# Cross-attention with layer norm: scores from high and low query parts, masks converted once and spread through DRAM

## The reference

```python
Q, K, V = heads(x @ wq.T + bq), heads(ctx @ wk.T + bk), heads(ctx @ wv.T + bv)
scores = where(mask == 0, -1e9, Q @ K.T / 4)
out = (softmax(scores) @ V).merged() @ wo.T + bo + x
out = (out - mean) * rsqrt(var + 1e-5) * gamma + beta
```

## Time and profile before

| what | value |
|---|---|
| median of three runs | 165.19 us (164.49, 165.19, 167.47) |
| the profiled execution's own time | 164.33 us |
| its span | 162.5 us |
| busy in the span: PE / DVE / ACT / POOL | 137.3 / 124.9 / 94.7 / 115.5 us |
| mean granted TensorE clock | 0.964 of full |

### The profile page before, as it was taken

The page is one execution under the profiler, slowest core; times in us unless marked ns, Lnnn a source line. Parts: engine busy times, 40 slices in busy tenths (PEclk is TensorE's granted clock), DMA queues, the critical chain, the costliest instruction groups (busy, mean ns, idle before and its releaser), DMA issues.

```text
span 162.5 us, 2904 instructions
## 1 busy us (share of the span) xinstructions
PE 137.3 (84%) x992; PEld 87.0 (54%) x992; DVE 124.9 (77%) x231; ACT 94.7 (58%) x166; POOL 115.5 (71%) x111
## 2 busy tenths in 40 slices
PE   0798975989899998999899989998999579999400
PEld 0676853746556655565556565655665335468300
DVE  0263899348788897989798979898989797999951
ACT  3349687593963666766676675846763815640220
POOL 5003741029999539999999999999981899667783
PEclk9999999699999999999999999999999999999955
DMA  4988983999927886006730940048003503003024
GB/s 119 342 234 198 283 197 85 317 244 269 287 71 187 314 217 252 0 0 196 180 148 0 224 167 0 2 105 274 12 2 76 187 0 129 0 4 122 7 94 166
DMA packets 10175, 23.21 MB, mean 143 GB/s; under 512 B 1584, under 2 KB 1840, under 8 KB 10160
## 3 DMA queue, kind: packets, MB, share of 16 engines
q1 hardware_dynamic: 9584, 22.03, 46.7%
q10 hardware_dynamic: 576, 0.99, 1.9%
HBM read 14.62 MB, written 4.19 MB: 116 GB/s over the span
## 4 chain that ended last, share of the span: by engine, by line
PE 45%; DVE 15%; POOL 14%; issue 7%; DMA 7%; SPq 6%; ACT 3%; POOLq 1%; DVEq 0%
PE ps_w L436 11%; PE ps_w L357 9%; PE ps_w L331 8%; DMA m_sb<-maskT 7%; PE ps_s L385 6%; PE ps_s L412 5%; POOL y L873 5%; DVE nmax L667 4%; POOL y L876 4%; DVE turned L688 3%; SPq L215 3%; PE ps_s L391 3%; ACT y L585 2%; DVE cn L701 2%; POOL rstd L857 2%
## 5 line engine op out<-in xcount | busy, mean ns | idle before, releaser
L667 DVE TENSOR_REDUCE nmax<-ps_w 128x8 f32<-128x512 f32 x56 | 37.7, 678 | 15.2 <-PE ps_w L357 14.8
L572 ACT ACTIVATE probs<-ps_s 128x512 f32<-128x512 f32 x64 | 33.1, 602 | 18.3 <-PE ps_s L396 18.3
L810 POOL TENSOR_TENSOR xt_l<-xt_sb,xt_h 128x1024 fp32r<-128x1024 f32 x7 | 16.6, 2374 | 30.6 <-ACT xt_h L533 19.8
L436 PE MATMUL ps_w<-wo_sb,cn 128*128 128x256 f32 x112 | 29.3, 387 | 3.9 <-DVE cn L701 3.6
L357 PEld LDWEIGHTS ps_w<-k_half,q_mask 128*128 128x128 f32 x112 | 17.3, 190 | 25.5 <-DVE nmax L667 19.7
L357 PE MATMUL ps_w<-k_half,q_mask 128*128 128x256 f32 x112 | 27.9, 335 | 3.2 <-DVE nmax L667 2.9
L436 PEld LDWEIGHTS ps_w<-wo_sb,cn 128*128 128x128 f32 x112 | 19.3, 189 | 9.2 <-DVE cn L701 5.5
L585 ACT ACTIVATE y<-res,shift,rstd 128x256 f32<-128x256 f32 x28 | 14.8, 590 | 12.6 <-POOL shift L859 12.5
L873 POOL TENSOR_TENSOR y<-y,brow 128x512 f32<-128x512 f32 x14 | 17.9, 1279 | 4.5 <-ACT y L585 4.1
L688 DVE STREAM_TRANSPOSE turned<-ps_s 128x1024 f32<-128x1024 f32 x16 | 19.8, 1240 | 0.8 <-PE ps_s L412 0.8
L844 POOL TENSOR_TENSOR x_sb<-x_sb,brow 128x1024 f32<-128x1024 f32 x8 | 19.1, 2382 | 0.1
(11 more groups left out here) (75 smaller groups left out, 203.3 us busy)
## 6 DMA issues: line engine op xcount, KB each, us to landing
m_sb<-maskT SPq DMA_DIRECT2D x32, 128.0 KB, 3.5
q_mask<-mask SPq DMA_DIRECT2D x32, 128.0 KB, 2.6
x_sb<-x SPq DMA_DIRECT2D x8, 512.0 KB, 4.3
xt_sb<-xT SPq DMA_DIRECT2D x7, 512.0 KB, 4.4
out<-y SPq DMA_DIRECT2D x6, 512.0 KB, 3.4
xt_sb<-xT SPq DMA_DIRECT2D x2, 256.0 KB, 5.7
out<-xt_sb SPq DMA_DIRECT2D x2, 256.0 KB, 2.0
brow<-bias_rows SPq DMA_DIRECT2D x1, 384.0 KB, 6.4
```

The lines of the kernel that those rows point to most:

```text
L436: return pe.matmul(tile_outputs(c, i)[:, t], cn[:, c % 2, j, (2 * i + t) * P:(2 * i + t + 1) * P], wo_sb[:, j], start=j == 0 and c < LAST, ...
L572: act.activation(probs[:, g % 2, quad], ps_s[:, quad], ACT.Exp).then_inc(e_done, 1)
L667: dve.tensor_reduce(nmax[:, c % 2, t].rearrange("p (q r) -> p q r", r=32)[:, :, 2 * j:2 * j + 2], max_bank(c, i).rearrange("p (q h k) -> p ...
```

## The change

- **Masks of chunks 3 to 7.** They are loaded once (64 keys, as two halves of the queries on 128 partitions by 256 columns), converted by one VectorE instruction in step s for chunk s + 3, behind divide(s - 1, 1) and ahead of maxima 4; written to a tensor `masks` in DRAM, and read back from there to `mask` (four transfers) and to `q_mask` (two). GpSimd's `mask_values` is gone, and so are `load_mask` and `copy_mask` for these chunks.
- **Mask of chunk 0** comes in a second copy (`m_first`) that VectorE writes straight into `q_mask`, by two instructions; `copy_mask(0)` is gone. Mask 2 and the value blocks move on VectorE behind maxima(1, 2) of step 0.
- **Scores from chunk 2** use high and low parts of queries and keys, as float32r: three products of four quads each in place of the float32 product. The high parts are ACT copies (`queries_high` twice a chunk, `keys_high` once), the low parts GpSimd differences (`queries_low`, `keys_low`).
- **Values** are projected per batch and per head parity, 16 float32 products of 64 x 128 in place of 8 of 128 x 256, all ahead of max_scores(0, 0); the bias is added by two instructions in place of five.
- **ACT** makes the high part of chunk 1 ahead of the first queries. **SP** loads xT(1) and wv ahead of mask 0.
- **Ends:** in TensorE's step 7 output(5, 1) stands ahead of values(6, 1); on VectorE moments(5, 0) come behind maxima(7, 7), and residual and moments (5, 1) ahead of divide(6, 1); on GpSimd the last chunk's first deviations come ahead of deviations(6, 2:4).

```diff
@@ -214,6 +238,31 @@
                     sp.dma_start(m_sb[quad_rows(quad), c % 2], maskT[c].rearrange("(a k) n -> k a n", a=2)
                                  ).then_inc(in_mask[c % 2], 16)
+
+            def load_once(c):
+                if c >= SPREAD_FROM + 2:
+                    sp.wait_ge(once_done, c - 1 - SPREAD_FROM)
+                for u in range(2):
+                    sp.dma_start(m_once[rows(u), c % 2], maskT[c, :, u * COLS:(u + 1) * COLS]).then_inc(in_once[c % 2], 16)
+
+            def mask_away(c):
+                sp.wait_ge(once_done, c + 1 - SPREAD_FROM)
+                for u in range(2):
+                    sp.dma_start(masks[c, :, u * COLS:(u + 1) * COLS], mask_once[rows(u), c % 2].bitcast(F32)
+                                 ).then_inc(mask_out[c % 2], 16)
+
+            def spread_mask(c):
+                n = (c - SPREAD_FROM) // 2 + 1
+                sp.wait_ge(mask_out[c % 2], 32 * n)
+                sp.wait_ge(max_done, HALVES * (c - 1))
+                for half in range(2):
+                    sp.dma_start(q_mask[rows(1 - half), c % 2, half].bitcast(F32),
+                                 masks[c].unsqueeze(1).to_broadcast([64, 2, CHUNK])).then_inc(beside_in[c % 2], 16)
+                if c >= NM:
+                    sp.wait_ge(s_done, PAIRS * (c - NM + 1))
+                for quad in range(QUADS):
+                    sp.dma_start(mask[quad_rows(quad), c % NM].bitcast(F32),
+                                 masks[c].rearrange("(a k) n -> k a n", a=2)).then_inc(mask_in[c % 2], 16)
...
@@ -245,10 +294,11 @@
             load_first_xt(0)
             load_first_xt(1)
+            for half in range(2):
+                sp.dma_start(m_first[rows(half)], maskT[0]).then_inc(in_mfirst, 16)
+            load_xt(1)
+            sp.dma_start(wv_sb[:], wv).then_inc(in_wv, 16)
             load_mask(0)
-            sp.dma_start(wv_sb[:], wv).then_inc(in_wv, 16)
-            load_xt(1)
-            copy_mask(0)
             load_mask(1)
...
@@ -259,16 +309,19 @@
             sp.dma_start(brow[:, 1:4], bias_rows[:, 1:4].to_broadcast([P, 3, D])).then_inc(in_rows, 16)
             sp.dma_start(wo_sb[:], wo).then_inc(in_wo, 16)
-            load_mask(3)
+            load_once(3)
             load_xt(4)
-            load_mask(4)
+            load_once(4)
             load_x(1)
+            mask_away(3)
             for s in range(1, CHUNKS):
                 if s + 4 < CHUNKS:
                     load_xt(s + 4)
-                    load_mask(s + 4)
+                    load_once(s + 4)
                 if s + 2 < CHUNKS:
-                    copy_mask(s + 2)
+                    spread_mask(s + 2)
+                if s + 3 < CHUNKS:
+                    mask_away(s + 3)
                 if s + 1 < CHUNKS:
...
@@ -287,18 +340,20 @@
                     for d in range(PC):
                         mm = pe.matmul(ps_w[:, 1, j * 256:j * 256 + 256], wk_sb[:, d, j * P:(j + 1) * P],
-                                       ctx_t[:, d, 0:BATCHES], start=d == 0, stop=d == PC - 1)
+                                       ctx_t[:, d], start=d == 0, stop=d == PC - 1)
                 mm.then_inc(k_done, 1)
-            def project_values(b):
-
-                if b == 0:
-                    pe.wait_ge(in_wv, 16)
-                for d in range(PC):
-                    mm = pe.matmul(value_bank(b)[:, 0, (b % 2) * 256:(b % 2) * 256 + 256],
-                                   ctx_t[:, d, b:b + 2].rearrange("p b k -> p (b k)"), wv_sb[:, d],
-                                   start=d == 0, stop=d == PC - 1)
-                mm.then_inc(v_done, 1)
+            def project_values():
+
+                pe.wait_ge(in_wv, 16)
+                for b in range(BATCHES):
+                    for d in range(PC):
+                        for h in range(2):
+                            mm = pe.matmul(projected_values(h)[:, b], ctx_t[:, d, b],
+                                           wv_sb[:, d].rearrange("p (q e) -> p q e", e=32)[:, :, 16 * h:16 * h + 16],
+                                           start=d == 0, stop=d == PC - 1)
+                            if d == PC - 1:
+                                mm.then_inc(v_done, 1)
...
@@ -380,11 +440,26 @@
                     pe.wait_ge(qe_done, g + 1)
                     pe.wait_ge(e_done, QUADS * g)
-                for quad in range(QUADS):
-                    r = quad_rows(quad)
-                    pe.matmul(ps_s[:, quad], k_pair[r, b, j].rearrange("p h k -> p (h k)"), q_sb[r, c % NQ, j],
-                              start=True, stop=False)
-                pe.wait_ge(mask_done, c + 1)
+                if c < PARTS_FROM:
+                    for quad in range(QUADS):
+                        r = quad_rows(quad)
+                        pe.matmul(ps_s[:, quad], k_pair[r, b, j].rearrange("p h k -> p (h k)"), q_sb[r, c % NQ, j],
+                                  start=True, stop=False)
+                else:
+                    pe.wait_ge(kh_done, 1)
+                    pe.wait_ge(kl_done, 1)
+                    pe.wait_ge(qh_done, g + 1 - 2 * PARTS_FROM)
+                    for n, (k, q) in enumerate(((k_high, q_high), (k_low, q_high), (k_high, q_low))):
+                        if q is q_low:
+                            pe.wait_ge(ql_done, g + 1 - 2 * PARTS_FROM)
+                        for quad in range(QUADS):
+                            r = quad_rows(quad)
+                            pe.matmul(ps_s[:, quad], k[r, b, j].rearrange("p h k -> p (h k)"), q[r, c % 2, j],
+                                      start=n == 0, stop=False)
+                if c < SPREAD_FROM:
+                    pe.wait_ge(mask_done, c + 1)
+                else:
+                    pe.wait_ge(mask_in[c % 2], 16 * QUADS * ((c - SPREAD_FROM) // 2 + 1))
                 for a in range(2):
...
@@ -460,11 +535,8 @@
             project_keys()
             project_first_queries()
-            project_values(0)
-            project_values(1)
-            project_values(2)
+            project_values()
             max_scores(0, 0)
-            project_values(3)
             max_scores(0, 1)
...
@@ -477,9 +549,9 @@
                 scores(s, 0)
                 if s == LAST:
-                    values(LAST - 1, 1)
                     output(LAST - 2, 1, 0)
                     output(LAST - 2, 1, 1)
+                    values(LAST - 1, 1)
                     scores(LAST, 1)
...
@@ -612,6 +693,8 @@
                 if s < LAST:
                     queries_beside(s + 1, 1)
+                if PARTS_FROM <= s + 1 < CHUNKS:
+                    queries_high(s + 1, 1)
                 if s == 0:
...
@@ -624,6 +707,9 @@
                 if s + 2 < CHUNKS:
                     queries_beside(s + 2, 0)
+                    if s == 0:
+                        keys_high()
+                    queries_high(s + 2, 0)
                 if s == LAST:
...
@@ -669,16 +755,15 @@
             def value_blocks():
-                dve.wait_ge(v_done, BATCHES)
+                dve.wait_ge(v_done, 2 * BATCHES)
                 dve.wait_ge(fill_done, 5)
                 dve.wait_ge(in_bv, 16)
-                for h, b, n, first in ((0, 0, 2, 0), (0, 2, 2, 2), (1, 0, 2, 1), (1, 2, 1, 3), (1, 3, 1, 0)):
+                for h in range(2):
                     r, e = rows(h), slice(16 * h, 16 * h + 16)
                     dve.tensor_tensor(
-                        v_bd[r, first:first + n, :, e],
-                        value_bank(b)[r, 0].rearrange("k (b p e) -> k b p e", b=2, e=32)[:, b % 2:b % 2 + n, :, e],
+                        v_bd[r, :, :, e], projected_values(h),
                         brow[r, 0].rearrange("k (p e) -> k p e", e=32)[:, :, e].unsqueeze(1)
-                        .to_broadcast([64, n, PAIRS, 16]), ALU.add).then_inc(vbd_done, 1)
+                        .to_broadcast([64, BATCHES, PAIRS, 16]), ALU.add).then_inc(vbd_done, 1)
...
@@ -734,13 +819,28 @@
             def scaled(i):
                 c = LAST
-                dve.wait_ge(ln_done, deviations_done(LAST - 1, True) + 2 * (i + 1))
+                dve.wait_ge(ln_done, deviations_done(c, i == 1))
                 dve.wait_ge(beta_done, 1)
                 dve.wait_ge(last_gam_done, 2 * (i + 1))
                 for t in (2 * i, 2 * i + 1):
                     dve.scalar_tensor_tensor(y_of(c)[:, t], y_of(c)[:, t], rstd[:, c % 2, t:t + 1], beta(),
                                              ALU.mult, ALU.add).then_inc(last_bet_done, 1)
+            def first_mask_values():
+                dve.wait_ge(in_mfirst, 32)
+                for half in range(2):
+                    r = rows(1 - half)
+                    dve.tensor_scalar(q_mask[r, 0, half], m_first[r].unsqueeze(1).to_broadcast([64, 2, CHUNK]), 0.0, -BIG,
+                                      ALU.is_equal, ALU.mult).then_inc(mfirst_done, 1)
+
+            def mask_values_once(c):
+                n = (c - SPREAD_FROM) // 2
```

(55 more changed lines are left out.)

53 lines of the change are left out of this document (42 added, 11 removed).

## The result

The changed kernel takes 181.33 us (median of four, 180.78 to 182.49) against 165.34 for the kernel before on the same chip: a ratio of 1.0995, 95% interval 1.0915 to 1.1075. The prediction was 179.0 us, with slower at 0.93. The profiled execution took 181.49 us, its span is 179.7, so 17.2 us have come on top of the 164.33 of the one before.

A forecast was written before the change was run, and what follows sets the result against it. It took a loop through VectorE and TensorE, 16.21 us a step, as the bound. From 164.33, -0.95 + 8.2 + 4.8 + 0.5 + 2.2 gave 179.1, say 179.0 us; range 171 to 185.

The forecast's parts named there:

- Mask 3 in step 0: VectorE's first `mask_values_once` waits for mask 3, issued late on SP's queue: loss 6.5 us, +8.2 with clock and front.
- quick landing: Rival: mask 3, 128 KB in place of 512, lands quickly; +8.2 falls to +2.8, total 173.7 us; chance 0.12.
- The front: Up to the first scores: no `copy_mask(0)` wait and values in column pairs give -0.7 us (bounds -1.5, +0.5).
- Half clock: After step 0's stall, TensorE works another 3.41 us stretch at a granted clock of 0.50: +1.7 us.
- Conversions beside GpSimd: Steps 1 to 4: VectorE's mask conversion waits for GpSimd's instruction to end, +4.8 us (bounds 0.4 and 10).
- The rival that nobody holds them: GpSimd does not hold the conversions; steps cost 0.4 us, step 0 is 0.7 shorter, total 174.0; chance 0.13.
- The masks' way through DRAM: DRAM round trip of masks 4 to 7 has most of a step before it is read: 0 us.
- Scores in parts: Float32r rounds save TensorE 0.38 us a group, 4.6 over twelve; -0.95 us reaches the end (bounds 0, -4.6).
- TensorE is not the bound: Denies the rival that TensorE is the bound and all 4.6 us reach the end, 175.4; chance 0.11 with tail.
- `neg` late by 0.5: Half_keys in step 4 make deviations(2) late, and ACT's normalising then holds `neg` up: +0.5 us (bounds 0, 2).
- GpSimd's tail and the ends: GpSimd's list from step 6 ends later, +2.2 us (bounds 0, +3); the other ends count 0 (-1, +1).
- Other side: Rival: mask 3 is there near 29.6, step 0 has no stall, -4.0 for +8.2, total 166.9 us; chance 0.04.

## Why the prediction was right

**Mask 3 in step 0: right, and undersized.** Predicted for start and step 0 together +8.2, measured 11.0. The way was as written: mask 2 later, SP's copies later, mask 3 issued at 35.03 (predicted 32.3), landed at 42.16 (39.4), conversion held by low_x(3) for about a microsecond (1.03; predicted 1.1), first scores of step 1 at 49.48 (46.7). Of the 2.8 us between the two, 1.7 were there when mask 2 was done (29.43 against 27.7), and the rest is the queue, where mask 3 follows mask 2 by 5.6 in place of 4.65. Moving it ahead of the copies, moving mask 2's copies behind it, and doing mask 2 earlier each took its share of step 0 away (9.9, of which 5.2 came back in step 1, 8.6 and 3.7 us of the 24.94). The bound of +2.8 for a quick landing leaves out the conversion itself, 0.35; nothing hung on it.

**The front: the step that failed.** I took -0.7 for everything up to the first scores; it was +1.1. Mask 0 stands on VectorE where GpSimd has just started low_x(1): 2.71 us in place of 0.69. I had read just that from mask 2, used it for steps 1 to 4 and not here, where a `low_x` was in GpSimd's list as well. A half-clock stretch at 17.4 came on top. The runs part the two: with neither the start is 21.9 to 22.1 (mask 0 moved, or begun ahead of low_x), with mask 0 held and no stretch 22.8 to 23.5, with both 24.4 to 25.0. So the rest of the front gave 1.4, twice what I took, the held conversion cost some 0.9 and the stretch, which no run explains, 1.6.

**Half clock: +1.7 predicted, about 2.2 measured.** The stretch lasted 13.65 us, but TensorE was busy for only 4.31 us of them (the last of the stretches above), so half of that, 2.2, was lost. The cost was nearly right, the picture of one more 3.41 us stretch was not, and in part it was luck: the old stretch at 28.03, which I had left standing, was gone (1.6 us of loss less), and the one at 17.4, which I had not in the sum, cost 1.7.

**Conversions beside GpSimd: right.** The predicted extra in steps 1 to 4 was 0.59, 0.59, 1.79, 1.79, less 0.19 each for scores: 0.4, 0.4, 1.6, 1.6 against +0.3, +0.1, +1.5, +1.5. Steps 3 and 4 are named by TensorE's wait for VectorE (1.41 us at 93.74) and by the 2.02 and 2.04 us. The rival that nobody holds them is out: the durations of one instruction follow those on GpSimd, a swap on GpSimd alone took both steps back to 16.0 and 16.3, and where VectorE began first it was GpSimd's instruction that became longer. The masks' way through DRAM, taken as 0, was 0: no wait in the changed kernel is put down to a landing from `masks`.

**Scores in parts: -0.95 predicted, about -0.4 measured.** The chain shows what TensorE spends on a group, three rounds and the mask's:

```profile
133.25 0.91 PE ps_s L457 x8
134.16 0.46 PE ps_s L466 x6
```

The three rounds take 0.91 in place of 1.07: 0.16 saved a group, not 0.38, about 2 us over twelve groups and not 4.6. I had priced a round at 0.23 from the mask's. Of it 0 to 0.2 us a step reach the end, 0.4 over steps 2 to 5. TensorE is not the bound: a step with 0.35 us less of its work was at most 0.2 shorter. What I had missed is that the parts cost more by the order of GpSimd's list than they give: without them steps 3 to 5 were 3.4 us shorter, though step 1 took 1.5 of it back.

**`neg` late by 0.5: right.** In step 5 it comes 0.39 after TensorE wants it (row at 118.30), because ACT's normalising waited 3.30 us for GpSimd's shift. The row of ACT:

```profile
115.11 2.08 ACT L666 ACTIVATE y<-res,shift,rstd 128x256 f32<-128x256 f32 x4 [3.30 <-POOL shift L969]
```

With GpSimd's order changed it was gone, -0.7.

**GpSimd's tail and the ends: the sum right, the parts not.** Predicted +2.2, measured 46.5 in place of 44.1 from step 6 on: +2.4. GpSimd waits 4.00 us in step 6, and its list ends at 177.23, 2.5 before the end, as 160.02 did before. But step 6 also has a stretch at half clock behind TensorE's wait of 1.99 us for `cn`, which no term had: it takes 17.31 us here and 15.64 to 15.90 in the three later kernels without that stretch. So about 1.4 of the 2.4 are the stretch, and that the sum fits is luck. With GpSimd's order changed the tail gave back 1.1 in place of the 2.4 expected, and VectorE became the last. The new ends were taken as 0, and were: they gain 0.26 in step 6 and lose 0.27 behind it.

**Other side.** I gave it 0.04 as luck of timing: 166.9 if the mask arrives before 30. With the orders of SP and GpSimd mended the time was back at that of the kernel before. But step 0 was then 12.43 us, 12.60 (no parts), 15.91 or 16.99, and 16.35 with SP's order alone, on both sides of the 15.03 before: mask 3 comes at about the moment when VectorE wants it, and tenths of a microsecond decide whether low_x(3) holds it. With both orders mended the clock fell behind it in one of these kernels and not in the others.

## What to carry to other kernels

Before moving an instruction in a list worked in order, write down what stands behind it on its own engine, and what stands behind each consumer of its result: here mask 2's conversion, cheap and not wanted for a step, held four copies, the wide rows and mask 3, and through them every engine. Where VectorE has a conversion that GpSimd can hold, place it by GpSimd's list: after a long instruction there, not under it; a swap of two GpSimd instructions gave 3.1 us in two steps. Where two such instructions start within a tenth of a microsecond of each other, either can win: compare kernels step by step before crediting an edit with the whole gain. And a saving on the engine that is busiest is worth only what its waits leave of it: 0.35 us of TensorE's work a step came to 0.2 at most.

## What the runs showed of the hardware

- The same conversion of 128 x 256 took 0.25 to 0.30 us with GpSimd idle or between its instructions, 1.25 beside an affine of 1.27, and 2.02 beside a `low_x` of 2.35. Which of the two starts first decides who waits. In the changed kernel low_x(1) began at 13.22 and mask 0 at 13.42, and mask 0 took 2.71, low_x 2.37; in the run without parts mask 0 began at 13.06 and low_x(1) at 13.10, and mask 0 took 0.69, low_x 2.89 (0.69 and 2.86 in the run with mask 2 at its old place). The Trainium skill, "SBUF — State Buffer", section "Who interferes with whom", says that the holder of the shared ports blocks the other for the whole instruction; by that rule the trace agrees, at three lengths.
- After TensorE waits of about 2 us its granted clock was at 0.50, the 1.2 GHz level, for 3.4 us in some kernels and stayed at 1.00 in others of nearly the same list. In step 6 it fell in the changed kernel and in eight others, and not in the one before nor in three, all with a wait of 1.8 to 2.0 us there. In step 3, behind a wait of 1.4 us, it fell in three kernels and not in the changed one nor in the one with mask 2 at its old place. Such a stretch made its step 1.2 to 1.7 us longer. What decides it in a given execution was not settled.
- In the long idle of step 0 (TensorE waits from 32.69 to 43.84) the clock fell to 0.50 at 34.50 and was back at 1.00 at 48.15, 4.3 us after TensorE took up work.
